# Second experts turned onto the gelu experts' plan, last products in row groups, and a new deal of routing steps in the dilated turn

## What is computed

```python
gate_logits = x @ gate_weight.T
top_vals, top_idx = jax.lax.top_k(gate_logits, TOP_K)
routing_w = jax.nn.softmax(top_vals, axis=-1)
mask = jnp.any(top_idx[:, :, None] == jnp.arange(E)[None, None, :], axis=1)
h = jax.nn.silu(jnp.einsum('td,efd->tef', x, w1))
counts = jnp.sum(mask, axis=0)
h_sum = jnp.einsum('tef,te->ef', h, mask.astype(h.dtype))
h_mean = h_sum / jnp.maximum(counts, 1)[:, None].astype(h.dtype)
y_mean = jnp.einsum('ef,edf->ed', h_mean, w2)
out = jnp.einsum('tk,tkd->td', routing_w, y_mean[top_idx])
```

## Time and profile before

| | |
|---|---|
| median of 3 runs | 3500.41 us |
| the profiled execution | 3499.89 us |
| its span, first to last instruction | 3498.1 us |
| mean granted TensorE clock | 0.904 of full |
| busy: PE / DVE / ACT / POOL | 81% / 63% / 44% / 29% of the span |

### The profile page before, as it was taken

One profiled execution on the slowest core, in us unless ns is written; L12 is line 12 of the kernel. 1 busy time (PEld: TensorE's weight loads), 2 busy tenths in 40 slices (PEclk: granted clock), 3 DMA queues, 4 the chain that ended last, 5 costly groups with the idle time before them and its releaser, 6 DMA issues. The chain is left out here.

```text
span 3498.1 us, 64431 instructions
## 1 busy us (share of the span) xinstructions
PE 2841.1 (81%) x20886; PEld 1554.3 (44%) x20887; DVE 2207.3 (63%) x4232; ACT 1550.4 (44%) x3274; POOL 1025.6 (29%) x1344
## 2 busy tenths in 40 slices
PE   6777869999999999999299767488888888629998
PEld 3334513433344333443199645355555555403336
DVE  6774567787777777774222245577777777527762
ACT  1112526666666666657155322344445444304440
POOL 0001311122222222222233366325566555610000
PEclk9998969999999999999699889888889898759995
DMA  2002462232322323220222123333233232031123
GB/s 78 0 0 85 174 126 40 37 56 39 53 47 40 55 39 53 47 40 8 83 61 61 54 94 105 106 60 62 58 64 60 59 63 56 24 99 52 51 67 109
DMA packets 209250, 215.73 MB, mean 62 GB/s; under 512 B 33456, under 2 KB 185200, under 8 KB 209008
## 3 DMA queue, kind: packets, MB, share of 16 engines
q1 hardware_dynamic: 183376, 176.63, 22.2%
q0 software_dynamic: 14336, 25.72, 2.8%
q10 hardware_dynamic: 11312, 10.35, 1.0%
HBM read 129.26 MB, written 81.90 MB: 60 GB/s over the span
## 5 line engine op out<-in xcount | busy, mean ns | idle before, releaser
L1536 ACT ACTIVATE attn_exps<-attn_sbank 128x392 f32<-128x392 f32 x1600 | 704.7, 503 | 465.4 <-PE attn_sbank L1453 460.7
L1581 DVE TENSOR_REDUCE attn_mx<-attn_rot 128x1 f32<-128x784 f32 x768 | 722.0, 967 | 188.3 <-PE attn_rot L1466 185.5
L1453 PE MATMUL attn_sbank<-attn_q,attn_k 99*128 99x392 bf16 x1536 | 450.1, 333 | 10.7 <-ACT attn_exps L1536 9.5
L1466 PE MATMUL attn_rot<-attn_k,attn_q 96*128 96x392 bf16 x1536 | 401.8, 344 | 69.5 <-DVE attn_mx L1581 39.2
L2282 ACT ACTIVATE dil_exps<-dil_sbank 128x512 f32<-128x512 f32 x512 | 289.3, 597 | 364.6 <-PE dil_sbank L2180 361.1
L2338 DVE TENSOR_REDUCE dil_mx<-dil_rot 128x4 f32<-128x1024 f32 x256 | 307.3, 1218 | 74.2 <-PE dil_rot L2190 72.2
L1493 PE MATMUL attn_acc<-attn_exps,attn_v 128*32 128x392 f32 x3584 | 350.8, 503 | 0.0
L1453 PEld LDWEIGHTS attn_sbank<-attn_q,attn_k 99*128 99x128 bf16 x1536 | 148.8, 98 | 269.8 <-ACT attn_exps L1536 134.5
L2654 PE MATMUL silu_ph<-silu_route_w,silu_xT 128*128 x424 | 238.0, 645 | 21.3 <-issue 12.6
L2190 PE MATMUL dil_rot<-dil_k,dil_q 96*128 96x256 bf16 x1024 | 174.9, 300 | 81.6 <-DVE dil_mx L2338 50.4
L1466 PEld LDWEIGHTS attn_rot<-attn_k,attn_q 96*128 96x128 bf16 x1536 | 117.4, 98 | 276.2 <-DVE attn_mx L1581 179.0
(11 more groups left out here) (367 smaller groups left out, 4804.3 us busy)
## 6 DMA issues: line engine op xcount, KB each, us to landing
attn_q<-q_pieces SPq DMA_DIRECT2D x192, 98.0 KB, 3.5
attn_k<-k_pieces SPq DMA_DIRECT2D x192, 98.0 KB, 4.9
silu_x<-silu_rows SPq DMA_DIRECT2D x212, 64.0 KB, 1.8
dil_q<-dil_q_pieces SPq DMA_DIRECT2D x192, 66.0 KB
dil_k<-dil_k_pieces SPq DMA_DIRECT2D x192, 66.0 KB
q_pieces<-qkv_piece SPq DMA_DIRECT2D x16, 588.0 KB, 3.1
k_pieces<-qkv_piece SPq DMA_DIRECT2D x16, 588.0 KB, 3.2
v_rows<-qkv_v SPq DMA_DIRECT2D x16, 476.0 KB, 3.8
```

The costliest lines, as they stand in the source:

```text
L1453: ins = nc.tensor.matmul(into[:, 0:HS], k_[t.side][g][:, j, c * P:(c + 1) * P], q[t.side][g][:, j, cols], start=True, stop=True)
L1466: ins = nc.tensor.matmul(rot[b][:, hf, 0:HS], q[nxt.side][g][0:QROWS, j, c * P:(c + 1) * P], k_[nxt.side][g][0:QROWS, j, cols], start=True ...
L1536: nc.scalar.activation(e_[:, n % NP, :], sbank[(n + t.side) % 3][:, 0:HS], ACT.Exp, scale=A_DIM ** -0.5).then_inc(s_ex, 1)
L1581: nc.vector.tensor_reduce(into, rot[b][:, :, 0:HS], AX.XY, ALU.max).then_inc(s_free, 1)
```

## The change

Four parts, in the order of the program. (1) `route_tail` takes a semaphore for each early load. The first mixture's second layer has its own now, and the second mixture's second layer (16 x 256 KB) is loaded here too, on ACT's queue behind the first layer, into memory of its own. (2) In the dilated turn `place` 5 to 10 come one per head at h = 2 to 7, where all stood at h=2; `gate` and `store` come at h=8, where they stood at 4 and 5; `pick` n comes at h = 12 + n // 4, where it was 11 + (n + 2) // 4. (3) `experts_silu` follows the first mixture's plan: POOL copies `w1[e]`, 128x512, into one of four buffers `ws`; PE makes four products of 128 columns with these as weights; ACT takes silu in two halves of 256 columns; DVE reduces 128x4x128 to `part`, 128x4; and POOL adds `part` of tile t-2 into `sums[e]` ahead of the copy for tile t+3. The sum over tokens is then done when the tiles are; `acc`, its zeroing and the 64 products with ones go. The last product is in four column groups of 32, and one product with `same` adds them and repeats the result in four row groups. (4) `finish` has no hardware loop, and four images' products stand in four row groups of PE (partitions 32j to 32j+15).

```diff
@@ dilated_attention, route_steps and steps
         if h >= 2:
             out.append(("scatter", h - 2, lag))
-        if h == 2:
-            out += [("place", n, lag) for n in range(5, 11)]
-        return out + {4: [("gate", lag)], 5: [("store", lag)]}.get(h, [])
+        if 2 <= h <= 7:
+            out.append(("place", h + 3, lag))
+        if h == 8:
+            out += [("gate", lag), ("store", lag)]
+        return out
...
-                out += [("pick", n) for n in range(16) if 11 + (n + 2) // 4 == h] + [("root",)] * (h == 12)
+                out += [("pick", n) for n in range(16) if 12 + n // 4 == h] + [("root",)] * (h == 12)
@@ experts_silu, POOL (new)
+                def copy(n, at):
+                    e = pool.value_load(table[0:1, 1, at], min_val=0, max_val=E - 1)
+                    nc.gpsimd.tensor_copy(ws[n][:], w1[:, bass.ds(e, 1), :].rearrange("p o n -> p (o n)")).then_inc(s_ws, 1)
+
+                def tile(t):
+                    if 2 <= t.lo <= NT + 1:
+                        e = pool.value_load(table[0:1, 1, bass.ds(t.t - 2, 1)], min_val=0, max_val=E - 1)
+                        pool.wait_ge(s_part, t.t - 1)
+                        pool.wait_ge(s_sum, t.t - 1)
+                        into = sums[:, bass.ds(e, 1), :].rearrange("p o c -> p (o c)")
+                        nc.gpsimd.tensor_tensor(into, part[(t.lo - 2) % NX][:], into, ALU.add).then_inc(s_sum, 1)
+                    if t.lo + AHEAD < NT:
+                        if t.lo >= 1:
+                            pool.wait_ge(s_ph, 4 * t.t)
+                        copy((t.lo + AHEAD) % NX, bass.ds(t.t + AHEAD, 1))
@@ experts_silu, PE
-                        e = pe.value_load(table[0:1, 1, bass.ds(t, 1)], min_val=0, max_val=E - 1)
-                        nc.tensor.matmul(ph[n][:, :], xT[n][:], w1[:, bass.ds(e, 1), :].rearrange("p o f -> p (o f)"), start=True, stop=True).then_inc(s_ph, 1)
+                        pe.wait_ge(s_ws, t + 1)
+                        for c in range(4):
+                            nc.tensor.matmul(ph[n][c // 2][:, c % 2 * TILE:(c % 2 + 1) * TILE], ws[lo % NX][:, c * P:(c + 1) * P], xT[n][:], start=True, stop=True).then_inc(s_ph, 1)
...
-                for e in range(E):
-                    for c in range(4):
-                        ins = nc.tensor.matmul(psum_[:, 4 * e + c:4 * e + c + 1], acc[:, e, c * P:(c + 1) * P], onesc[:], start=True, stop=True)
...
-                        ins = nc.tensor.matmul(pm[0:E, 0:P], mean[:, e, c, :], w2[:, e, c, :], start=(e == 0 and c == 0), stop=(e == E - 1 and c == 3))
+                        ins = nc.tensor.matmul(pm[32 * c:32 * c + 32, 0:P], mean[:, e, c, :], w2[:, e, c, :], start=(e == 0), stop=(e == E - 1))
+                pe.wait_ge(s_y4, 1)
+                nc.tensor.matmul(pr[:, 0:P], same[:], y4[:], start=True, stop=True).then_inc(s_rep, 1)
@@ experts_silu, ACT and DVE
-                        nc.scalar.activation(h[n][:], ph[n][:, :], ACT.Silu).then_inc(s_h, 1)
+                            nc.scalar.activation(hT[lo % NX][:, 2 * k:2 * k + 2, :].rearrange("p c n -> p (c n)"), ph[n][k][:, 0:2 * TILE], ACT.Silu).then_inc(s_h, 1)
...
-                nc.vector.memset(acc[:], 0.0)
-                        e = dve.value_load(table[0:1, 1, bass.ds(t - 1, 1)], min_val=0, max_val=E - 1)
-                        nc.vector.tensor_tensor(part, h[1 - n][:], part, ALU.add).then_inc(s_acc, 1)
+                        nc.vector.tensor_reduce(part[(lo - 1) % NX][:], hT[(lo - 1) % NX][:], AX.X, ALU.add).then_inc(s_part, 1)
@@ finish, PE
-                with pe.Fori(0, B // 4) as i:
-                    for j in range(4):
-                        pe.wait_ge(s_add, 4 * i + j + 1)
-                        for h in range(2):
-                            ins = nc.tensor.matmul(pa[j][:, h, 0:HS], ymean[:], gates_t[:, 4 * i + j, h * HS:(h + 1) * HS], start=True, stop=True)
+                for i in range(B // 4):
+                    for h in range(2):
+                        for j in range(4):
+                            if i > 0 and h == 0:
+                                pe.wait_ge(s_add, 4 * i + j - 3)
+                            ins = nc.tensor.matmul(pa[j][:, h, 0:HS], ymean[32 * j:32 * j + SILU.n, :], gates_t[32 * j:32 * j + SILU.n, i, h * HS:(h + 1) * HS], start=True, stop=True)
```

More of the change, by code:

```diff
@@ L1096, in pool_done, with route_tail @@
             pool.wait_ge(self.s_sct[j], self.SCT * PAIRS)
-def route_tail(nc, a, ex, xs, table, keep, stage, early, s_early, positions=None, counts=None):
+def route_tail(nc, a, ex, xs, table, keep, stage, early, positions=None, counts=None):
     E, K, NT = ex.n, ex.picks, ex.tiles
@@ L2582, in experts_silu @@
         two = range(2)
-        w2 = w1[:, :, :].rearrange("p e (c d) -> p e c d", c=4)
-        acc = m.sb("acc", [TILE, E, FF])
         ident = m.sb("ident", [P, P])
-        only = m.sb("only", [P, E, E])
-        onesc = m.sb("onesc", [P, 1])
+        only = m.sb("only", [P, E, 32])
+        same = m.sb("same", [P, P])
         cnt = m.sb("cnt", [P, E])
         rcnt = m.sb("rcnt", [P, E])
-        scaled = m.sb("scaled", [P, E, E])
+        scaled = m.sb("scaled", [P, E, 32])
         sums = m.sb("sums", [P, E, 4])
-        mean = m.sb("mean", [P, E, 4, E])
+        mean = m.sb("mean", [P, E, 4, 32])
+        part = [m.sb(f"part{n}", [P, 4]) for n in range(NX)]
+        y4 = m.sb("y4", [P, P])
+        ws = [m.sb(f"ws{n}", [P, FF]) for n in range(NX)]
         x = [m.sb(f"x{n}", [TILE, P]) for n in range(NX)]
         xT = [m.sb(f"xT{n}", [P, TILE]) for n in two]
-        h = [m.sb(f"h{n}", [TILE, FF]) for n in two]
+        hT = [m.sb(f"hT{n}", [P, 4, TILE]) for n in range(NX)]
         px = [m.ps(f"px{n}", [P, BANK]) for n in two]
-        ph = [m.ps(f"ph{n}", [P, BANK]) for n in two]
-        psum_ = m.ps("psums", [P, BANK])
+        ph = [[m.ps(f"ph{n}{k}", [P, BANK]) for k in two] for n in two]
         pm = m.ps("pm", [P, BANK])
+        pr = m.ps("pr", [P, BANK])
         s_w = m.sem("weights")
-        s_w2 = m.sem("w2_loaded")
-        s_z = m.sem("zeroed")
+        s_ws = m.sem("ws_copied")
         s_x = [m.sem(f"x_loaded{n}") for n in range(NX)]
@@ L2625, in _ @@
                 run_tiles(sp, NT, tile)
-                sp.dma_start(gates_t[:], gates_d).then_inc(s_gates, 16)
-                sp.wait_ge(s_ph, NT)
-                for e in range(E):
-                    sp.dma_start(w2[:, e], a["L3_w2"][e].rearrange("(c f) d -> f c d", c=4)).then_inc(s_w2, 16)
-                sp.wait_ge(s_gates, 16)
+                for g in range(4):
+                    sp.dma_start(gates_t[32 * g:32 * g + E, :, :], gates_d.rearrange("e (i g) s -> e g i s", g=4)[:, g]).then_inc(s_gates, 16)
+                sp.wait_ge(s_gates, 16 * 4)
+            @block.gpsimd
+            def _(pool):
+                def copy(n, at):
[12 more added lines that the diff above has]
+                        copy((t.lo + AHEAD) % NX, bass.ds(t.t + AHEAD, 1))
+                nc.gpsimd.memset(sums[:], 0.0).then_inc(s_sum, 1)
+                pool.wait_ge(s_early, 16 * E)
+                for t in range(AHEAD):
+                    copy(t, slice(t, t + 1))
+                run_tiles(pool, NT, tile)
             @block.tensor
             def _(pe):
-                pe.wait_ge(s_w, 32)
-                pe.wait_ge(s_early, 16 * E)
+                pe.wait_ge(s_w, 16 * 3)
                 def turn(t, lo, x_loads):
@@ L2901, in layouts @@
         d[f"tiles{ex.n}"] = np.pad(np.arange(ex.tiles, dtype=np.float32).reshape(-1, rows).T, ((0, P - rows), (0, 0)))
-    d["only"] = np.eye(SILU.n, dtype=np.float32).reshape(1, -1)
+    d["only"] = np.eye(SILU.n, 32, dtype=np.float32).reshape(1, -1)
+    d["same"] = (k[:, None] % 32 == k[None, :] % 32).astype(np.float32)
     return {n: np.ascontiguousarray(x) for n, x in d.items()}
```

112 lines of the change are left out of this document (58 added, 54 removed).

## The result

The changed kernel takes 3507.84 us in the median of 20 runs, the kernel before 3499.61 in 20 runs beside it: a ratio of 1.0023, with a 95% interval of 1.0013 to 1.0033. It is slower by about 8 us. The forecast was 3484, faster. The profiled execution has a span of 3507.1 us, 9.0 over before.

The account below looks back on a forecast made before the run. Limits were read by stage: SP's loads pace the second mixture's tiles, PE bounds finish, DVE and PE one half each of the dilated turn. 3499.89 - 40 + 75 + 0 - 31 - 20 = 3484 us, range 3410 to 3535.

Parts of the forecast that it names:

- POOL's queue becomes the bound: Second mixture's tiles: two register loads with arithmetic in POOL's queue take 1.65 us per tile, over SP's 1.279.
- The term of +75: Second mixture's 212 tiles: slower by 75 us through POOL's queue, bounds +15 to +180.
- Behind the tiles: From the last tile's product to the copied vectors: 14.6 us in place of 45.4, so -31.
- in finish: Final stage: with four row groups side by side, 29.3 us in place of 49.4, so -20.
- The start of the stage: Second mixture's start: dropped zeroing set against competing loads and waits for POOL's copies, 0 (-4 to +6).
- the term of the deal: Dilated stage's redealt routing steps: 2.5 us saved per turn over 16 turns, -40 (0 to -70).
- the wait of L917: Dilated turn: DVE stands still 1.61 us for POOL's squares; a maximum placed ahead of L917 fills it.
- POOL's pair is dearer: Rival, tiles: POOL's register loads cost more, 21 us per 0.1 us per tile, slower from 1.73; chance 0.16.
- The deal brings little: Rival, dilated stage: PE gets waits in the second half, -8 in place of -40, 3516 us; chance 0.10.
- POOL not binding: Rival, tiles: POOL's queue doesn't bind, +75 shrinks to 0 or 15, 3409 to 3424 us; chance 0.19.
- row groups giving nothing: Rival, finish: row groups don't run beside each other, finish stays at 49 us, 3504 us; chance 0.14.
- a register load of 600 ns: Tiles: the skill page's floor for a tensor_load, giving 2.27 us per tile and 3615 us; chance 0.02.

Follow-up runs that it names:

- experiment 2: Changed kernel with POOL adding into a constant slot, 3424.4 us; with the expert's number kept in a register, 3422.3 us; and also without SP's bounds check, 3357.4 us.
- experiment 3: Changed kernel with finish's products all in the first row group of PE (partitions 0 to 15): 3523.6 us, ratio 1.007 to the kernel before.
- two picks alone: Kernel before with only picks 0 and 1 one head later: 3500.9 us, ratio 1.000.

## Why the prediction was wrong

**Where it held.** "POOL's queue becomes the bound" is what happened, and its price, 1.65 us per tile, was 1.69. The prediction had itself worked out 0.17 us for a pair in the loop and then put in 0.15; with 0.17 the sum gives 1.69. The term of +75 came out at +83.6, and one register load less takes all of it back (experiment 2). Behind the tiles -35 for -31, in finish -22 for -20, with the row groups shown by experiment 3. The start of the stage is +0.5 for 0, the early load's 3.8 against the 3.3 by which the first product comes earlier behind the first DMA. Had the deal brought its 40, the kernel would have been at 3490 us, for 3484 predicted and 3500 before; with L867 in its old place it is 3477.

**The step that failed** is the term of the deal, "I take 2.5 ... **-40**". It came out at -22, or -23.5 alone, and with the 18 us that are missing the sum turned from faster to slower. I costed the instructions that DVE gets and loses, and I read DVE's list only. The pick on which POOL's L867 hangs moved a head later, past `take`'s two additions on POOL, and L947 with it came to lie beside it. That place alone cost about 30 us. Without it the deal is worth 50 to 53 us, inside the bounds I gave (0 to -70) and above what I took.

Within the term, its parts were also put down wrongly. I credited up to 1.6 us per turn to the wait of L917. By itself its end brings nothing in time (two picks alone: 1.000), since the turn is held further on, at the bunch of places. The places are the gain: 3.1 us in an undisturbed turn (47.76 to 44.64), where I had counted 2.8 us of DVE work. Of these 2.8, moreover, 0.77 doesn't go elsewhere but vanishes: L1049 takes 0.93 us in the bunch, beside a POOL addition, and 0.16 where it stands now. What the gain has beside it is the clock. Before, in each turn, PE stood nearly still while DVE did the bunch, and then got half the clock:

```profile
2614.60:2617.60 3.00, 0.84 (x7) 0.55 (x7) 2.93 (x6) 0.70 (x2) 2.25 (x3) 1.00 0.12 33
2617.60:2620.60 3.00, 2.88 (x42) 1.75 (x46) 1.88 (x4) 0.38 (x1) 1.55 (x2) 0.52 0.42 66
```

PE was busy 0.84 of 3 us at the full clock, and in the next 3 us the granted clock was 0.52, between its two levels of 1.2 and 2.4 GHz and near the lower; the fall comes 23.8 to 24.1 us after L854 in 12 of the 13 full turns. With the places dealt that hole is gone. How much of the 3.1 us is DVE's work and how much the clock is not separated. In the changed kernel the same stretch of a long turn (first two lines) and of a short one (last two):

```profile
2562.70:2565.70 3.00, 1.72 (x11) 1.27 (x11) 2.76 (x6) 1.56 (x5) 2.35 (x3) 0.81 0.51 69
2565.70:2568.70 3.00, 3.00 (x44) 1.94 (x45) 1.87 (x5) 1.10 (x3) 2.25 (x4) 0.62 0.13 33
2610.00:2613.00 3.00, 1.71 (x15) 1.28 (x14) 2.77 (x6) 1.75 (x4) 2.37 (x3) 1.00 0.33 55
2613.00:2616.00 3.00, 2.78 (x63) 1.81 (x66) 2.28 (x5) 1.39 (x3) 2.24 (x4) 1.00 0.13 33
```

PE's busy time in the first 3 us is the same, 1.72 and 1.71, and the clock fell in one of them and not in the other; the long turn loses 2.5 us from there on. From 2564.5 to 2567.9 its granted clock is 0.51, and in the same stretch of the short turn 1.00. Among the kernels with places dealt, the medians of where a turn's seventh maximum comes after L854 go with the number of long turns: at 17.6 to 17.7 us none or one of 13 full turns was long (the three kernels with L947 short and picks dealt), at 17.9 four were (places alone), at 18.1 six to nine (the eight with L947 long). So L947's 2.2 us cost a short turn little directly, 0.2 to 0.4 us, and the rest goes with more turns being long. But the seventh maximum doesn't decide it: in the changed kernel it comes at 18.09 us in short turns and in long ones alike. What differs there is where the clock stood against the turn: its first fall came 6.3 to 6.7 us after L854 in the four short turns, and 6.0 to 6.2 in five of the nine long ones, 8 us or later in the others but the first. What decides whether the clock falls again is not shown.

**The rivals.** "POOL's pair is dearer" had the right sign and was right by 0.04 us only; its turning point of 1.73 was not reached. "The deal brings little" is what tipped the sum, with the half of its gain gone and not four fifths, and not by the mechanism I gave: PE hardly got new waits in the second half (2.6 us idle there before, 2.6 in a long turn and 3.1 in a short one of the changed kernel), POOL's instruction came into the first. It had a chance of 0.10, and slower as a whole 0.26; the time of 3508 lies inside the range. POOL not binding and row groups giving nothing were both refuted, and so was a register load of 600 ns: POOL's takes 288 in the changed kernel too. Between the forecast of -16 and the +9 of the profile lie 25 us: 18 are the deal's. Of the rest, +9 on the tiles and +4 before the dilated turns, which kernels alike up to there also differ by, go the same way; against them stand -6 behind the tiles and in finish.

**On the pages.** The Trainium skill, TensorE: Matmul & The Clock Gate, Part 3, gives a measured 3.07 for four row tiles, of 32 rows and 512 columns. Here, with 16 rows and 392 columns, 16 passes took 1.60 us at a granted clock of 1.00 (changed kernel) against 0.65 us each at 0.50 (experiment 3), a factor of 6.5. If the clock counts for 2 of it, which is an estimate, the groups give 3.3: near the page's figure. For L947 the fitting sentence is in GPSIMD Engine Reference, Key points: GpSimd shares its SBUF interfaces with VectorE, and contends with DVE instructions with two SBUF inputs. L947 has two; 0.26 us alone and 2.48 us beside POOL's instruction agree with that. The page gives no size.

## What to carry to other kernels

A step that several engines carry out has a place in each engine's list. When a table of steps is dealt anew, compare every list, and look for what a long instruction of POOL now lies beside on DVE: here one place on POOL was worth 31 us, and no count of instructions showed it.

An engine that is under half busy can still set the pace by its queue. Count register loads, address arithmetic and starts per turn of the loop, take their price from a loop that has them, and hold a value in a register rather than load it twice (86 us here). Then do the same for the next queue: another 65 us lay in SP's bounds check, in the two mixtures together.

A wait that ends earlier is worth nothing until the next place that holds the turn goes too (in the stage: two picks alone -1 us, places alone -38, both -53).
